# Gated graph network, 2048 nodes: the first two chunks' gates as block products over both chunks, and operands loaded one by one

## The chip, the cores and the metric

One NeuronCore of one Trainium2 chip. The metric is the device time of one execution in microseconds, the median of the runs shown.

## What is computed

Five steps of a gated graph network on 2048 nodes with 256 features, then a small head, a residual and a layer norm. Each step is, with A the 0/1 adjacency matrix:

```
a_in  = A   @ (state @ in_W.T  + in_b)
a_out = A.T @ (state @ out_W.T + out_b)
a = concat([a_in, a_out, state])
r = sigmoid(a @ r_W.T + r_b);  z = sigmoid(a @ z_W.T + z_b)
h_hat = tanh(concat([a_in, a_out, r * state]) @ h_W.T + h_b)
state = (1 - z) * state + z * h_hat
```

The end is out = layernorm(x + tanh(state @ o1_W.T + o1_b) @ o2_W.T + o2_b).

## The kernel before, in words

The input and output weights are folded into the gates' weights, so a step is an adjacency part, y = A state and A.T state, and a gate part. The state stands transposed in `state_t`: two feature tiles of 128 rows, 2048 nodes in columns, in four chunks of 512 (chunks 0 to 3). All arithmetic that must be exact to fp32 is split into a high and a low f16 half: a product is then three passes over (high, high), (high, low), (low, high), `PASSES`. The biases that pass through A become a degree row times a vector; ScalarE seeds a gate's PSUM bank with one direction's (`seed`, L490) and VectorE adds the other's (`degree_part`, L831).

**Adjacency part (steps 1 to 4).** Four groups a step: group g has direction g % 2 (0 is A.T, which feeds the second weight block) and chunk pair g // 2. A group multiplies a 2 x 2 block matrix by a 2 x 2 block matrix with seven block products instead of eight (Strassen's scheme in Winograd's form). The products are named P1, P6, P5, P7, P3, P2, P4 after their semaphores, in TensorE's order in `group`; each is 16 matmuls 128 x 128 by 128 x 512 (`product`, L1173) from the turned state rows `xop` and the fp8 matrix block sums. ScalarE copies P1 (L536), VectorE adds the products up to the four corners y11, y22, y12, y21 (L1012 to L1031), and each corner is split into halves by ScalarE (`y_hi`, L554) and VectorE (`y_lo`, L1038). P1, P2 share bank A; P6, P7, P4 bank B; P5 has bank E, P3 bank C. `first_group` is group 0 of a step in another order, since the state rows of chunk 3 reach `xop` last: 36 matmuls on the early rows, 4 of P1, 12 of P3, P2, 4 of P6, 4 of P5, P7, 4 of P3, P4. P2 there waits for the copy of P1, P7 for VectorE's first sum.

**Operands.** The seven matrix block sums of each group lie in DRAM (`kept`, 3.67 MB a group). Each of two SBUF places holds a whole group: SP (`load_group`, L310) loads group at + 2 in two DMAs when P4 of group at is done. SP also issues the DMA transposes that turn new state rows into `xop` (`turn_rows`, L324), in the same queue. In step 0 the raw blocks were stored by SP (`store_raw`, L301 and L303).

**Gate part.** `gates(t, c)` for one chunk: six tiles (r, z, h by two feature tiles), each of 6 blocks x 3 passes = 18 matmuls (`gate_tile`, L1260), in three banks in turn. ScalarE applies sigmoid or tanh (L476), VectorE forms r * state (L837), z's part and the new state (L848, L854, L857). Beside the last tiles of a chunk the next chunk's banks are seeded, in the last chunk (c = 3) those of the next step. The new state is split for the gates (`split_hi` L447, `split_lo` L777), and its rows and the block sums of them are split for the transposes (`rows_hi` L464, L468; `row_sums` L821 to L826; `rows_lo` L803 to L810).

**Order of a step.** first_group, group 1, gates of chunks 0 and 1, groups 2 and 3, gates of chunks 2 and 3. Every engine's program is written out by hand in that order, and each engine works strictly in its order.

Of the kernel before, what the change touches and what calls it, by code (L numbers as in the profile page):

```python
# [15 lines left out]
P = 128  # L16
N = 2048
D = 256
STEPS = 5
# [29 lines left out]
Y_SPLIT = {False: {"y22": 1, "y12": 2, "y11": 3, "y21": 4}, True: {"y11": 1, "y22": 2, "y12": 3, "y21": 4}}  # L49
# [6 lines left out]
def gnn_program(nc, x, x_t, adj, adj_t, io_w, gate_w, o_w, bias, o2_b, out):  # L56
    ctx = ExitStack()
    with ctx:
# [6 lines left out]
        def need(eng, s, value):  # L65
            if value > 0:
# [11 lines left out]

        tg_words = PAIRS * NX * CW // 4
        slot_w = [areg[:, d * half:d * half + tg_words].rearrange("p (m w) -> p m w", m=PAIRS) for d in range(2)]  # L80
        slot8 = [areg[:, d * half:d * half + tg_words].bitcast(F8).rearrange("p (m s n) -> p m s n", m=PAIRS, s=NX)
                 for d in range(2)]
# [22 lines left out]
        sum_1, sum_u, sum_v = [pq_words[:, slot_words + i * CW:slot_words + (i + 1) * CW] for i in range(3)]  # L105
# [14 lines left out]
        rs16 = tmp[:, 6 * CW:8 * CW].bitcast(F16).rearrange("p (s f n) -> p s f n", s=2, f=FT)  # L120
        ring_b = tmp[:, 8 * CW:12 * CW].rearrange("p (r w) -> p r w", r=2)
# [7 lines left out]
        vdeg = sb("vdeg", [P, 2, GT], F32)  # L129
        mx = sb("mx", [P, 12], F32)  # L130
# [9 lines left out]
        gate_bank = bank[4:7]  # L140

# [23 lines left out]
        s_slot = [sem("s_slot0"), sem("s_slot1")]  # L165
        s_p1, s_p6, s_p5, s_p7, s_p3, s_p2, s_p4 = [sem(f"s_prod{i}") for i in (1, 6, 5, 7, 3, 2, 4)]
        s_sum1, s_sumu, s_u4, s_sumv = sem("s_sum1"), sem("s_sumu"), sem("s_u4"), sem("s_sumv")
        s_y22, s_y12, s_y21 = sem("s_y22"), sem("s_y12"), sem("s_y21")
        s_yh, s_yl = sem("s_yh"), sem("s_yl")
        s_gate = sem("s_gate")  # L170
# [21 lines left out]
        def pq_slot(t, c):  # L192
            return c if t == 0 else 2 + c % 2
# [66 lines left out]
        def _(sp):  # L260
# [45 lines left out]
            def load_group(t, g):  # L306
                d = g % 2
                for h in range(2):
                    ms = slice(h * PAIRS // 2, (h + 1) * PAIRS // 2)
                    sp.dma_start(slot_w[d][:, ms, :], kept[g][:, ms, :]).then_inc(s_slot[d], 16)  # L310
# [23 lines left out]
            load_group(1, 0)  # L334
# [9 lines left out]
            load_group(1, 1)  # L344
            for t in range(1, STEPS):
                for g in range(4):
                    at = 4 * (t - 1) + g
                    if at + 2 < 4 * LAST:
# [1004 lines left out]
```

## Time and profile before

| | us |
|---|---|
| median of 3 runs | 1029.72 |
| lowest, highest | 1029.61, 1030.45 |
| the profiled execution | 1030.75 |
| its span | 1028.9 |
| TensorE busy in the span | 1005.5 (98%) |
| VectorE busy | 592.3 (58%) |
| ScalarE busy | 403.8 (39%) |
| granted TensorE clock, mean | 0.992 of full |

The span runs from the first to the last instruction of one profiled execution; the profiled execution's own time lies 1.85 us above its span. A matmul's listed duration overlaps its neighbours'; what counts is the distance from one start to the next.

### The profile page before, as it was taken

The page shows a single profiled execution, that of the slowest core. Times are in us where ns is not written, and L with a number is a line of the kernel's source. Part 1 is how long each engine was busy: PE and PEld are TensorE (multiplying, and loading weights), DVE is VectorE, ACT ScalarE, POOL GpSimd, SP SyncE. Part 2 cuts the span into 40 slices and gives each one's busy share as a digit, 9 for nine tenths or more (in the row PEclk, how much of TensorE's full clock was granted, in tenths as well). Part 3 has the DMA queues.
Part 4 walks back from the last instruction along what each step waited for, and adds up shares of the span by engine and source line. Part 5 has one row for each costly group of instructions (what it writes and reads, how often), then busy time and mean ns, then how long its engine had stood idle before and what let it go on. Part 6 is the DMA issues. An engine that isn't in the chain of part 4 may idle for free.

```text
span 1028.9 us, 11463 instructions
## 1 busy us (share of the span) xinstructions
PE 1005.5 (98%) x4648; PEld 458.5 (45%) x4648; DVE 592.3 (58%) x933; ACT 403.8 (39%) x544; POOL 38.7 (4%) x43
## 2 busy tenths in 40 slices
PE   6999999999999999999999999999999999999995
PEld 3444444444444444444444444444444444444443
DVE  4999968895354338544433674353347534446756
ACT  3656665542144126413421552143135314322443
POOL 0311000000000000000000000000000002001100
PEclk8999999999999999999999999999999999999998
DMA  9998991327430244333003642410344335001101
GB/s 330 389 411 344 396 343 33 77 65 218 151 136 0 103 166 91 72 143 143 1 1 143 189 72 72 169 73 0 143 154 72 62 143 189 1 1 42 42 1 41
DMA packets 87236, 134.30 MB, mean 131 GB/s; under 512 B 60432, under 2 KB 75408, under 8 KB 78992
## 3 DMA queue, kind: packets, MB, share of 16 engines
q1 hardware_dynamic: 84880, 125.19, 35.8%
q0 software_dynamic: 2304, 8.39, 2.1%
q8 instruction: 36, 0.59, 0.2%
q14 instruction: 16, 0.13, 0.0%
HBM read 102.11 MB, written 16.78 MB: 116 GB/s over the span
## 4 chain that ended last, share of the span: by engine, by line
PE 92%; DVE 3%; ACT 2%; DMA 1%; issue 1%; SPq 1%; ACTq 0%; DVEq 0%
PE bank L1260 42%; PE bank L1173 36%; PE bank L1116 11%; PE bank L1292 1%; DMA tmp<-in_adj 1%; PE bank L1273 1%; DMA xop_words<-pq_words 0%; SPq L270 0%; DVE pq_words L810 0%; ACT pq_words L468 0%; DVE pq_words L1012 0%; DVE areg L957 0%; ACT pq_words L554 0%; ACT tmp L476 0%; DVE tmp L704 0%
## 5 line engine op out<-in xcount | busy, mean ns | idle before, releaser
L1173 PE MATMUL bank<-areg,xop_words 128*128 128x512 fp8e4 x1792 | 390.1, 379 | 1.4 <-DVE pq_words L1012 1.1
L1260 PE MATMUL bank<-pq_words,w 128*128 128x512 f16 x1440 | 327.3, 379 | 0.0
L1173 PEld LDWEIGHTS bank<-areg,xop_words 128*128 128x128 f16 x1792 | 174.5, 98 | 214.7 <-DVE pq_words L1012 3.1
L1260 PEld LDWEIGHTS bank<-pq_words,w 128*128 128x128 f16 x1440 | 140.9, 98 | 169.9 <-DVE pq_words L1038 0.2
L476 ACT ACTIVATE tmp<-bank,bias_sb,scal 128x512 f32<-128x512 f32 x120 | 93.1, 776 | 201.4 <-PE bank L1260 201.4
L554 ACT ACTIVATE pq_words<-pq_words 128x512 f16<-128x512 f32 x48 | 30.2, 630 | 236.8 <-DVE pq_words L1024 140.5
L831 DVE SCALAR_TENSOR_TENSOR bank<-deg_words,vdeg,bank 128x512 f32<-128x512 f16 x120 | 90.0, 752 | 51.8 <-ACT bank L490 50.7
L1260 PE MATMUL bank<-split,w 128*128 128x512 f16 x480 | 116.7, 379 | 2.4 <-issue 1.9
L1116 PE MATMUL bank<-areg,xop_words 128*128 128x512 fp8e4 x512 | 113.5, 385 | 3.7 <-ACT areg L421 3.7
L490 ACT ACTIVATE bank<-deg_words,vdeg 128x512 f32<-128x512 f16 x120 | 82.7, 691 | 5.2 <-DVE deg_words L794 1.5
L1116 PEld LDWEIGHTS bank<-areg,xop_words 128*128 128x128 f16 x512 | 50.7, 99 | 66.0 <-issue 7.4
L421 ACT ACTIVATE areg<-tmp 128x2048 fp8e4<-128x2048 int32 x32 | 61.1, 1910 | 37.3 <-DMA tmp<-in_adj_t 18.9
L1260 PEld LDWEIGHTS bank<-split,w 128*128 128x128 f16 x480 | 46.7, 98 | 59.7 <-issue 2.4
L1260 PE MATMUL bank<-tmp,w 128*128 128x512 f16 x240 | 58.3, 379 | 0.0
L837 DVE TENSOR_TENSOR tmp<-tmp,state_t 128x512 f32<-128x512 f32 x40 | 27.6, 690 | 51.4 <-ACT tmp L476 51.3
L1038 DVE SCALAR_TENSOR_TENSOR pq_words<-pq_words 128x512 f16<-128x512 f32 x48 | 33.2, 692 | 33.4 <-ACT pq_words L554 33.4
L854 DVE TENSOR_TENSOR tmp<-tmp 128x512 f32<-128x512 f32 x40 | 27.6, 690 | 38.5 <-ACT tmp L476 38.5
L404 POOL TENSOR_TENSOR areg<-areg,diag_words 128x256 f32<-128x256 f32 x16 | 15.8, 1020 | 724.4 <-DMA areg<-in_x 724.4
L1038 DVE SCALAR_TENSOR_TENSOR pq_words<-bank,pq_words 128x512 f16<-128x512 f32 x16 | 11.1, 691 | 53.7 <-ACT pq_words L554 53.7
L777 DVE SCALAR_TENSOR_TENSOR split<-state_t,scal,split 128x1024 f16<-128x1024 f32 x23 | 30.1, 1308 | 13.7 <-ACT split L447 13.7
L1260 PEld LDWEIGHTS bank<-tmp,w 128*128 128x128 f16 x240 | 23.5, 98 | 28.3
L482 ACT ACTIVATE tmp<-tmp,scal 128x512 f16<-128x512 f32 x40 | 28.9, 722 | 11.2 <-DVE tmp L837 9.9
(132 smaller groups left out, 602.9 us busy)
## 6 DMA issues: line engine op xcount, KB each, us to landing
areg<-kept_operands SPq DMA_DIRECT2D x32, 1792.0 KB, 10.6
tmp<-in_adj SPq DMA_DIRECT2D x16, 1024.0 KB, 7.0
tmp<-in_adj_t SPq DMA_DIRECT2D x16, 1024.0 KB, 8.3
kept_operands<-xop_words POOLq DMA_DIRECT2D x11, 512.0 KB, 8.2
areg<-in_x SPq DMA_DIRECT2D x8, 512.0 KB, 8.1
kept_operands<-areg SPq DMA_DIRECT2D x4, 1024.0 KB, 10.2
kept_operands<-tmp POOLq DMA_DIRECT2D x5, 512.0 KB, 3.3
pq_words<-in_gate_w SPq DMA_DIRECT2D x6, 384.0 KB, 6.2
```

The costliest lines, as they stand in the source:

```text
L421: nc.scalar.activation(raw8[k // JT][:, k % JT, :], stage[:, k % STG, :], ACT.Copy, accum_out=degc[:, k // JT, k % JT:k % JT + 1], saturat ...
L476: nc.scalar.activation(dst[:, gi % FT, :], gate_bank[gi % 3][:, :], ACT.Tanh if gi >= 2 * FT else ACT.Sigmoid, bias=bias_sb[:, 4 + gi:5 + ...
L482: nc.scalar.activation(rs16[:, 0, f, :], r_buf[:, f, :], ACT.Identity, scale=SIG).then_inc(s_rsh, 1)
L490: nc.scalar.activation(gate_bank[gi % 3][:, :], deg[:, 0, cols(c)], ACT.Identity, scale=vdeg[:, 0, gi:gi + 1]).then_inc(s_c0, 1)
L554: nc.scalar.activation(dst, src, ACT.Copy, scale=PSC / XDOWN).then_inc(s_yh, 1)
L777: nc.vector.scalar_tensor_tensor(split[:, c % 2, 1, :, :], state_t[:, :, cols(c)], SIG, split[:, c % 2, 0, :, :], ALU.mult, ALU.subtract). ...
L831: nc.vector.scalar_tensor_tensor(slot, deg[:, 1, cols(c)], vdeg[:, 1, gi:gi + 1], slot, ALU.mult, ALU.add).then_inc(s_c1, 1)
L837: nc.vector.tensor_tensor(r_buf[:, f, :], r_buf[:, f, :], state_t[:, f, cols(c)], ALU.mult) \
L1038: nc.vector.scalar_tensor_tensor(rows[:, 1, :], src, PSC / XDOWN, rows[:, 0, :], ALU.mult, ALU.subtract).then_inc(s_yl, 1)
L1116: return nc.tensor.matmul(dst[:, :], state_n[:, j, part, feat(f)], adj8[:, j, cols(c)], start=j == 0 and part == 0, stop=j == JT - 1 and p ...
L1173: last = nc.tensor.matmul(dst[:, :], xop[:, m // 2, operand_block(xo, part, m % 2), :], slot8[g % 2][:, m, mo, :], start=first and m == pa ...
L1260: last = nc.tensor.matmul(dst[:, :], w16[:, k, wp, feat(gi)], rhs, start=False, stop=i == KT - 1 and (wp, xp) == PASSES[-1], skip_group_ch ...
```

## The change

For chunks 0 and 1 of steps 1 to 4 (groups 0 and 1) the gates' adjacency input is formed for both chunks together. For each gate (r, z, h) the weights (two blocks by two feature tiles) times y (two blocks by two chunks) is again a 2 x 2 block product, by the same seven-product scheme. Four banks hold the four output tiles. The products on the right need y11, y21, y22 and four sums t1 to t4 of y's corners, which VectorE now forms in each of the two groups; seven instead of four values are split into halves (`Y_ORDER`), y12 no longer. The weights' block sums (`ws`) are formed once, in step 1: VectorE adds high and low of a direction's weights (`weight_full`, 1536 elements a partition), forms four sums of 384, ScalarE rounds them to f16 (`weight_hi`, 1536), VectorE makes the low halves. The degree terms are seeded per bank, two of them with differences (`vdif`, `degd`). Inside a gate VectorE adds the four products up to the corner banks while TensorE goes on with the rest; ScalarE copies the first product and one sum. The state parts stay as they are, 6 matmuls a tile. States of chunks 0 and 1 are both split between groups 0 and 1. All splits now use one scale.

The matrix operands have one SBUF place each instead of two for whole groups; the second region holds the split y values. SP loads each operand of the next group (512 KB, in pieces of 512 B) as soon as the product that used it is done. The last chunk of a step no longer seeds the next step's banks; the banks of chunk 2 are seeded in group 3.

`Y_ORDER` is y11, y22, t1, t3, t2, y21, t4 in group 0 and y22, t3, y11, t1, t2, y21, t4 in group 1. The core of the diff:

```diff
+            def load_operand(at, mo, done):
+                if at > 0:
+                    sp.wait_ge(done, at)
+                sp.dma_start(place_w[:, mo, :, :], kept[at % 4][:, :, mo * CW // 4:(mo + 1) * CW // 4]) \
+                    .then_inc(s_place[mo], 16)
+            def load_group(at):
+                load_operand(at, M11, s_p1)
+                load_operand(at, MT2, s_p6)
...
-                        sp.wait_ge(s_p4, at + 1)
-                        load_group(t + (g + 2) // 4, (g + 2) % 4)
+                for at in range(4 * (t - 1) + 1, 4 * t + 1):
+                    if at < 4 * LAST:
+                        load_group(at)
...
-                    elif n + 1 < CH * STEPS and n + 1 != CH * LAST + 2:
-                        seed(n + 1, (c + 1) % CH, gi - 3)
+                    elif c < CH - 1:
+                        seed(n + 1, c + 1, gi - 3)
...
+                copy_p1(t, g)
+                if g == 1:
+                    for i in range(4):
+                        pair_seed(t, 0, i)
...
+                if g == 3:
                     for gi in range(2):
                         seed(CH * t + 2, 2, gi)
...
+                for name in Y_ORDER[g]:
+                    if t == 1 and g == 1 and name == "y11":
+                        weight_hi(1)
+                    y_hi(t, g, name)
+                    if g == 1 and name == "y21":
+                        pair_copy(t, 0)
...
+            def pair_gates(t):
+                pair_seed(t, 1, 0)
+                pair_base_21(t, 0)
+                for i in range(1, 4):
+                    pair_seed(t, 1, i)
+                for i in range(3):
+                    pair_act(t, 0, i)
+                    pair_reset_hi(t, i)
+                pair_act(t, 0, 3)
+                pair_copy(t, 1)
...
                 rows_hi(n, 1)
+                if t == 1:
+                    weight_hi(0)
                 group(t, 0)
-                split_hi(0, split_at(t, 0), CH * (t - 1) + 1)
+                split_hi(0, split_at(t, 0), CH * (t - 1) + 2)
+                split_hi(1, split_at(t, 1), CH * (t - 1) + 2)
                 group(t, 1)
-                gates(t, 0)
-                gates(t, 1)
+                pair_gates(t)
...
-                ahead = n + 1 < CH * STEPS and n + 1 != CH * LAST + 2
+                ahead = c < CH - 1
...
+                elif name == "t1":
+                    dve.wait_ge(s_yh, y_done(t, g, "y11"))
+                    dve.wait_ge(s_y12, at + 1)
+                    if g == 1:
+                        dve.wait_ge(s_d3, pair_at + 1)
+                    nc.vector.tensor_tensor(y_sum_at[g]["t1"], sum_u, bank_a[:, :], ALU.subtract).then_inc(s_d1, 1)
+                elif name == "t2":
+                    dve.wait_ge(s_d1, pair_at + 1)
+                    nc.vector.tensor_tensor(y_sum_at[g]["t2"], sum_v, y_sum_at[g]["t1"], ALU.subtract).then_inc(s_d2, 1)
...
+            def weight_full(d):
+                k = FT * (1 - d)
+                if d == 0:
+                    dve.wait_ge(s_gate, GT * CH)
+                else:
+                    dve.wait_ge(s_wsh, 1)
+                nc.vector.tensor_tensor(w_full, w16[:, k:k + FT, 0, :], w16[:, k:k + FT, 1, :], ALU.add) \
...
+                nc.vector.tensor_tensor(s1, a21, a22, ALU.add).then_inc(s_wsum, 1)
...
+                nc.vector.tensor_tensor(degd, deg[:, :, cols(1)], deg[:, :, cols(0)], ALU.subtract).then_inc(s_gdeg, 1)
...
+                if t == 1 and g == 1:
+                    weight_full(1)
...
                 sums_v(at)
-                y_sum(at, "y22")
+                if t == 1 and g == 1:
+                    weight_sums(1)
+                if g == 1:
+                    for i in range(4):
+                        pair_degree(t, 0, i)
+                y_sum(t, g, "y22")
                 y_lo(t, g, "y22")
-                y_sum(at, "y12")
+                y_sum(t, g, "y12")
+                if g < 2:
+                    if g == 0:
+                        y_sum(t, g, "t1")
+                        y_sum(t, g, "t3")
+                        y_lo(t, g, "t1")
+                        y_lo(t, g, "t3")
+                    else:
+                        y_sum(t, g, "t3")
+                        y_lo(t, g, "t3")
+                        if t == 1:
+                            weight_lo(1)
+                        y_sum(t, g, "t1")
+                        y_lo(t, g, "y11")
+                        y_lo(t, g, "t1")
+                    y_sum(t, g, "t2")
+                    y_lo(t, g, "t2")
+                    y_sum(t, g, "y21")
+                    y_sum(t, g, "t4")
+                    y_lo(t, g, "y21")
+                    y_lo(t, g, "t4")
+                    return
...
+            def pair_sum_u(t, gate):
+                unit, slots = 3 * (t - 1) + gate, pair_banks[gate]
+                dve.wait_ge(s_gp6, unit + 1)
+                dve.wait_ge(s_gs1, unit + 1)
+                nc.vector.tensor_tensor(sum_b, slots[1][:, :], sum_a, ALU.add).then_inc(s_gu, 1)
+            def pair_sum_12(t, gate):
+                unit, slots = 3 * (t - 1) + gate, pair_banks[gate]
+                dve.wait_ge(s_gp5, unit + 1)
+                dve.wait_ge(s_gu, unit + 1)
+                nc.vector.tensor_tensor(slots[1][:, :], slots[2][:, :], sum_b, ALU.add).then_inc(s_g12, 1)
+            def pair_sum_22(t, gate):
+                unit, slots = 3 * (t - 1) + gate, pair_banks[gate]
+                dve.wait_ge(s_gp7, unit + 1)
+                nc.vector.tensor_tensor(sum_a, slots[3][:, :], sum_b, ALU.add).then_inc(s_gv, 1)
+                dve.wait_ge(s_gv, unit + 1)
+                nc.vector.tensor_tensor(slots[2][:, :], slots[2][:, :], sum_a, ALU.add).then_inc(s_g22, 1)
...
+            def pair_gates(t):
+                pair_sum_u(t, 0)
+                pair_sum_12(t, 0)
+                pair_sum_22(t, 0)
+                pair_degree(t, 1, 0)
+                pair_degree(t, 1, 1)
+                pair_degree(t, 1, 2)
+                pair_degree(t, 1, 3)
+                for i in range(3):
+                    pair_reset(t, i)
+                    pair_reset_lo(t, i)
+                pair_reset(t, 3)
+                pair_sum_u(t, 1)
...
+                if t == 1:
+                    degree_differences()
+                    weight_full(0)
+                    weight_sums(0)
+                    weight_lo(0)
                 group(t, 0)
                 split_lo(0, split_at(t, 0))
+                split_lo(1, split_at(t, 1))
...
+                pe.wait_ge(s_place[mo], 16 * (at + 1))
...
+                if g == 1:
+                    pe.wait_ge(s_d1, 2 * (t - 1) + 1)
+                elif g == 2:
+                    pe.wait_ge(s_zh, FT * CH * t + 1)
+                else:
+                    pe.wait_ge(s_yl, y_done(t, 2, "y11"))
+                product(bank_a, at, X11, M11, every).then_inc(s_p1, 1)
                 need(pe, s_y21, at)
-                product(bank_b, g, XS2, MT2, every).then_inc(s_p6, 1)
+                if g == 2:
+                    pe.wait_ge(s_zh, FT * CH * t + 2)
+                product(bank_b, at, XS2, MT2, every).then_inc(s_p6, 1)
...
+            def pair_product(t, gate, dst, operand, weights):
+                for d in range(2):
+                    if gate == 0:
+                        pe.wait_ge(s_yl, y_done(t, d, [n for n in Y_PLACE if Y_PLACE[n] == operand][0]))
+                        if t == 1 and operand in (Y22, YT1, YT2, YT3):
+                            pe.wait_ge(s_wsl, d + 1)
+                    for wp, xp in PASSES:
+                        last = nc.tensor.matmul(dst[:, :], weights(d, wp), yop[:, d, operand, xp, :], start=False,
+                                                stop=False, skip_group_check=True)
+                return last
...
+                pe.wait_ge(s_c1, seeds + 1)
+                pair_product(t, gate, slots[0], Y11, block(0, 0)).then_inc(s_gp1, 1)
+                pe.wait_ge(s_c1, seeds + 2)
+                pair_product(t, gate, slots[1], YT2, block_sum(2)).then_inc(s_gp6, 1)
+                pe.wait_ge(s_c1, seeds + 3)
+                pair_product(t, gate, slots[2], YT1, block_sum(1)).then_inc(s_gp5, 1)
+                pe.wait_ge(s_c1, seeds + 4)
+                pair_product(t, gate, slots[3], YT3, block_sum(3)).then_inc(s_gp7, 1)
+                pe.wait_ge(s_gs1, unit + 1)
+                pair_product(t, gate, slots[0], Y21, block(0, 1))
+                pair_state(t, gate, 0)
+                pe.wait_ge(s_g12, unit + 1)
+                pair_product(t, gate, slots[1], Y22, block_sum(4))
+                pair_state(t, gate, 1)
+                pe.wait_ge(s_g22, unit + 1)
+                pair_state(t, gate, 2)
+                pe.wait_ge(s_g21, unit + 1)
+                pair_product(t, gate, slots[3], YT4, block(1, 1))
+                pair_state(t, gate, 3)
```

## Rows read from the trace of the kernel before

**Rows 1.** The page: busy time of TensorE, and the chain by engine.
```profile
PE 1005.5 (98%) x4648; PEld 458.5 (45%) x4648; DVE 592.3 (58%) x933; ACT 403.8 (39%) x544; POOL 38.7 (4%) x43
...
PE 92%; DVE 3%; ACT 2%; DMA 1%; issue 1%; SPq 1%; ACTq 0%; DVEq 0%
```

**Rows 2.** The chain of waits in order of time: start, us, what; step 1.
```profile
281.71 46.62 PE bank L1260 x216
328.33 48.35 PE bank L1173 x224
```

**Rows 3.** TensorE's waits: us in total, times, longest.
```profile
PE bank L1173 <- DVE pq_words L1012: 1.1, 4, 0.3
```

**Rows 4.** The chain of waits before step 1's first group.
```profile
225.46 0.69 ACT bank L490
...
233.53 0.66 DVE bank L831
```

**Rows 5.** TensorE's timeline: start, us, line, operation, count, idle before and what ended it.
```profile
21.20 110.62 PE L1116 MATMUL bank<-areg,xop_words 128*128 128x512 fp8e4 x500 [3.69 <-ACT areg L421]
...
138.18 1.46 PE L1260 MATMUL bank<-split,w 128*128 128x512 f16 x6 [1.90 <-issue]
...
232.22 7.93 PE L1173 MATMUL bank<-areg,xop_words 128*128 128x512 fp8e4 x36
240.40 8.81 PE L1173 MATMUL bank<-areg,xop_words 128*128 128x512 fp8e4 x40 [0.25 <-DMA xop_words<-pq_words]
```

**Rows 6.** VectorE's timeline at the end of step 0.
```profile
237.34 0.42 DVE L821 TENSOR_TENSOR diag_words<-state_t 128x256 f32<-128x256 f32 x1
...
238.47 0.42 DVE L826 TENSOR_TENSOR diag_words<-state_t,diag_words 128x256 f32<-128x256 f32 x1
...
240.51 1.28 DVE L810 SCALAR_TENSOR_TENSOR pq_words<-diag_words,scal,pq_words 128x1024 f16<-128x1024 f32 x1
```

**Rows 7.** Groups by line and shape, VectorE, then ScalarE: busy us, mean ns.
```profile
L707 DVE TENSOR_TENSOR xop_words<-areg 128x1024 fp8e4<-128x1024 fp8e4 x11 | 13.4, 1217 | 0.0
...
L421 ACT ACTIVATE areg<-tmp 128x2048 fp8e4<-128x2048 int32 x32 | 61.1, 1910 | 37.3 <-DMA tmp<-in_adj_t 18.9 <-DMA tmp<-in_adj 18.4
...
L447 ACT ACTIVATE split<-state_t,scal 128x1024 f16<-128x1024 f32 x23 | 26.1, 1133 | 0.4 <-DVE state_t L857 0.4
...
L536 ACT COPY pq_words<-bank 128x512 f32<-128x512 f32 x16 | 9.4, 585 | 26.0 <-PE bank L1173 26.0
```

**Rows 8.** Windows: stretch, length, busy of each engine, granted clock, DMA share, GB/s.
```profile
21.00:23.00 2.00, 1.80 (x5) 0.74 (x6) 1.96 (x5) 2.00 (x6) 0.00 (x0) 0.50 0.97 332
...
25.00:27.00 2.00, 2.00 (x8) 0.82 (x7) 2.00 (x5) 1.35 (x2) 0.00 (x0) 0.66 1.01 376
...
138.00:140.00 2.00, 1.82 (x9) 0.90 (x10) 2.00 (x5) 1.98 (x5) 0.00 (x0) 1.00 1.02 305
```

**Rows 9.** VectorE's timeline at the end of step 2's first group.
```profile
443.64 0.69 DVE L1024 TENSOR_TENSOR pq_words<-bank,pq_words 128x512 f32<-128x512 f32 x1 [2.53 <-PE bank L1173]
445.03 0.69 DVE L1038 SCALAR_TENSOR_TENSOR pq_words<-pq_words 128x512 f16<-128x512 f32 x1 [0.70 <-ACT pq_words L554]
445.64 0.68 DVE L1028 TENSOR_TENSOR pq_words<-bank,pq_words 128x512 f32<-128x512 f32 x1
...
448.06 0.69 DVE L1031 TENSOR_TENSOR pq_words<-bank,pq_words 128x512 f32<-128x512 f32 x1 [0.35 <-PE bank L1173]
```

**Rows 10.** ScalarE's timeline, the same place.
```profile
444.37 0.63 ACT L554 ACTIVATE pq_words<-pq_words 128x512 f16<-128x512 f32 x1 [5.77 <-DVE pq_words L1024]
```

**Rows 11.** SP's storing of one raw matrix block, 512 KB in 512 B pieces.
```profile
L301 SPq DMA_DIRECT2D kept_operands<-areg x4: 983/2513/4620, 116.6 to 133.2; - x4
...
DMA to landing us min/median/max: 8.5/9.7/12.5
```

**Rows 12.** Windows: the stretch of those stores, and step 1's groups.
```profile
127.00:138.00 11.00, 9.28 (x43) 3.85 (x41) 7.67 (x21) 6.85 (x13) 0.00 (x0) 1.00 1.07 362
...
232.20:281.70 49.50, 48.96 (x226) 21.77 (x225) 22.17 (x33) 10.29 (x15) 0.72 (x1) 1.00 0.54 185
```

More of the change, by code:

```diff
@@ L47 @@
 NX = 7
-Y_SPLIT = {False: {"y22": 1, "y12": 2, "y11": 3, "y21": 4}, True: {"y11": 1, "y22": 2, "y12": 3, "y21": 4}}
+Y11, Y21, Y22, YT1, YT2, YT3, YT4 = range(7)
+Y_ORDER = {0: ("y11", "y22", "t1", "t3", "t2", "y21", "t4"), 1: ("y22", "t3", "y11", "t1", "t2", "y21", "t4"),
+           2: ("y22", "y12", "y11", "y21"), 3: ("y22", "y12", "y11", "y21")}
+Y_BASE = (0, 7, 14, 18)
+Y_STEP = 22
+Y_PLACE = {"y11": Y11, "y21": Y21, "y22": Y22, "t1": YT1, "t2": YT2, "t3": YT3, "t4": YT4}
+PAIR_TILES = ((0, 0), (0, 1), (1, 1), (1, 0))
 TJOBS = [(d, m) for d in range(2) for m in range(PAIRS)]
@@ L164, in gnn_program @@
         s_raw = [sem("s_raw0"), sem("s_raw1")]
[L165 removed]
+        s_place = [sem(f"s_place{i}") for i in range(NX)]
         s_p1, s_p6, s_p5, s_p7, s_p3, s_p2, s_p4 = [sem(f"s_prod{i}") for i in (1, 6, 5, 7, 3, 2, 4)]
@@ L565, in group @@
-                y_hi(t, g, "y22")
-                y_hi(t, g, "y12")
-                if g > 0:
-                    y_hi(t, g, "y11")
-                y_hi(t, g, "y21")
-                if t == LAST and g == 3:
-                    seed(CH * t + 2, 2, 2)
+                for name in Y_ORDER[g]:
[4 more added lines that the diff above has]
+                        pair_copy(t, 0)
@@ L1055, in group, with pair_degree @@
                 y_lo(t, g, "y12")
-                if g > 0:
-                    y_lo(t, g, "y11")
-                if t == LAST and g >= 2:
+                y_lo(t, g, "y11")
+                if t == LAST:
                     residual(g - 2)
-                y_sum(at, "y21")
+                y_sum(t, g, "y21")
                 y_lo(t, g, "y21")
-                if t == LAST and g == 3:
+                if g == 3:
                     degree_part(CH * t + 2, 2, 2)
+            def pair_degree(t, gate, i):
+                slot = pair_banks[gate][i][:, :]
+                row, scale = pair_term(gate, i, 1)
+                dve.wait_ge(s_c0, GT * CH * t + 4 * gate + i + 1)
+                nc.vector.scalar_tensor_tensor(slot, row, scale, slot, ALU.mult, ALU.add).then_inc(s_c1, 1)
@@ L1217, in first_group @@
                 need(pe, s_y12, at)
-                product(bank_c, g, XS4, M22, early, final=False)
+                product(bank_c, at, XS4, M22, early, final=False)
                 pe.wait_ge(s_sum1, at + 1)
-                product(bank_a, g, X12, M21, every, first=False).then_inc(s_p2, 1)
+                product(bank_a, at, X12, M21, every, first=False).then_inc(s_p2, 1)
                 wait_turned(pe, 1, n)
-                product(bank_b, g, XS2, MT2, late, first=False).then_inc(s_p6, 1)
@@ L1227, in first_group @@
+                product(bank_c, at, XS4, M22, late, first=False).then_inc(s_p3, 1)
                 pe.wait_ge(s_y22, at + 1)
-                product(bank_b, g, X22, MT4, every, first=False).then_inc(s_p4, 1)
+                product(bank_b, at, X22, MT4, every, first=False).then_inc(s_p4, 1)
             def ready(t, c, k):
@@ new lines, in pair_state @@
+            def pair_state(t, gate, i):
+                f, c = PAIR_TILES[i]
+                gi = FT * gate + f
+                if gate == 0:
+                    pe.wait_ge(s_spl, split_at(t, c) + 1)
+                if gate == 2:
+                    pe.wait_ge(s_rsl, FT * CH * t + 4)
+                for k in range(FT):
+                    for wp, xp in PASSES:
+                        rhs = split[:, c, xp, k, :] if gate < 2 else rs_pair[:, c, xp, k, :]
+                        last = nc.tensor.matmul(pair_banks[gate][i][:, :], w16[:, 2 * FT + k, wp, feat(gi)], rhs,
+                                                start=False, stop=k == FT - 1 and (wp, xp) == PASSES[-1],
+                                                skip_group_check=True)
+                last.then_inc(s_gate, 1)
@@ L1314, in _ @@
                 group(t, 1)
-                gates(t, 0)
-                gates(t, 1)
+                for gate in range(3):
+                    pair_gate(t, gate)
                 group(t, 2)
```

343 lines of the change are left out of this document (259 added, 84 removed).

## The prediction

> **What bounds the kernel now.** I read the page's busy shares and chain first, then TensorE's waits, the chain by time, and the timelines of the engines beside it. TensorE is busy 98% of the span and holds 92% of the chain [rows 1]: this kernel is a stream of matmuls. In steps 1 to 4 the chunk-pair gates run 216 matmuls in 46.62 us without a gap, 0.2158 us from start to start, and two adjacency groups 224 in 48.35 us, the same pace [rows 2]. (A matmul is listed with 379 ns since neighbours overlap; the pace counts.) In the adjacency groups a VectorE sum holds TensorE up in four places, 1.1 us in all [rows 3]. So a matmul taken away is worth 0.2158 us, and the question is whether VectorE and ScalarE, with the work they are given for it, still keep ahead of TensorE.
>
> **Matmuls removed.** A pair of chunks took 2 x 6 gate tiles x 6 blocks x 3 passes = 216 matmuls. Now each of three gates takes four products of 2 directions x 3 passes (24), three more (18), and four state parts of 6 (24): 66, so 198 a pair. 18 fewer in each of four steps are 72 x 0.2158 = **15.5 us less**.
>
> **Seeds no longer made ahead in the last chunk's gates.** In step 0 the chain from the last state rows to the first group runs over such a seed on ScalarE and such a degree part on VectorE [rows 4] to the transpose that TensorE waits for: 36 matmuls from 232.22 would end at 239.99, the next starts at 240.40, a gap of 0.41 us [rows 5]. Without the two pieces (0.69 and 0.66 us, partly beside other waits) I make the rows 0.8 us earlier, so the gap goes: **0.4 us less**. In steps 1 to 4 that work is moved to beside the adjacency groups, where there are 3 us of slack.
>
> **Weight sums, first direction (step 1 only).** ScalarE's copy of the first product now stands behind its rounding of the weight sums, and that behind VectorE's making them; the product X12 x M21 waits for that copy. VectorE, from its last row piece (starts 240.51, 1.28 us long, now 0.8 earlier, ends 240.99) [rows 6]: two tiny differences 0.25; one of 1024 elements 1.14 and the weights' hi plus lo of 1536 elements 1.75 (by 1217 ns for 1024 and 0.42 us for 256 [rows 6, 7], some 1.04 ns an element; successors start 0.08 before an end); four sums of 384, where the four of 256 take from 237.34 to 238.89, 1.55, and 128 more elements each make 2.08. That ends at 246.2. ScalarE's 1536 elements cost 1.52 (1133 ns for 1024 and 1910 for 2048), the copy 0.58 [rows 7]: TensorE goes on at 248.3. It is ready after 36 + 4 + 12 matmuls, at 243.4. **4.8 us more.** From both sides: 3.4 if the f16 sources run faster than the rows of fp8 and f32, 5.9 if nothing comes earlier; I take the rows' own rate. The Trainium skill (VectorE: DVE Perf Modes, The perf-mode tier table) gives tensor_tensor on 16-bit data in SBUF twice the rate of fp32; by it the 1024-element f16 difference would cost some 0.5 us less and the stall would be 4.3. No row here has that form.
>
> **TensorE's clock after that stall.** After 3.69 us idle (to 21.2 us) the granted clock was 0.50, that is 1.2 GHz, until between 25 and 27 us (0.66 there), so about 5.2 us at half rate; after the 1.90 us idle to 138.18 it was 1.00 [rows 5, 8]. A stall of 4.8 us is beyond the first. Half of 5.2: **2.6 us more**; bounds 0 (the clock stays) and 3.4.
>
> **Seven splits instead of four in an adjacency group.** VectorE's tail of a group is a chain with ScalarE: a sum (0.69), ScalarE's high half (0.63), the low half, each 0.04 after its source; independent VectorE instructions start 0.61 apart, dependent ones so 0.73 [rows 9, 10]. On step 2's clock, first group: the y22 sum starts at 443.64 as before, its low half 445.03, the y12 sum 445.64. Then t1 446.36 to 447.05, t3 447.09, low t1 447.75, low t3 448.47, t2 449.08, low t2 (its high half ends 450.44) 450.47, and only then the y21 sum, 451.08 to 451.77. P7 ends at some 443.5, 4 + 16 matmuls behind it make 447.8; there group 1 begins (bank A is free before, at 447.05), and its second product wants bank B after 16 more, at 451.3. It must wait for the y21 sum, which formerly began at 448.06 [rows 9]. The wait is 0.5 us, in four steps **2.0 us more**; bounds 0 and 1.2 each. In group 1 what follows has cover: both state splits (some 1.2 us each by 1024 elements [rows 7], the second moved here from the gates) delay the first sum to 457.3, wanted at 458.7; four degree parts (0.66 us apart [rows 4]) end by 462.8, where product P7 ends at 462.2 and its sum is wanted at 469.1.
>
> **The gates begin without a cushion.** They began with six state matmuls and six of the first direction; now the second direction's y11 is their fourth matmul and t2 their tenth. Group 1 ends at 472.5. Low y11 is ready at 471.2, t2 at 474.0, wanted at 474.4: 0.4 us of cover. The first product's copy (475.8, wanted 477.7), low y21 (476.0), the first corner sum (478.5, wanted 480.3) have 2 us each. I followed the other two gates likewise: each runs 14.2 us, its copy and sums come 2 to 3 us early, seeds earlier still. The group behind waits for the second update's first product, which is over 2 us early. Cost 0, but where VectorE ran 1 us later in this stretch, each step would lose about 0.6.
>
> **Weight sums, second direction (step 1).** In group 1 VectorE also has 1.75 + 2.08 and, late, the low halves, 1.75; ScalarE 1.52. The y22 sum then comes 2.4 us after its product, and the low halves of the weights stand before t1. Low y11 is 0.2 us late, low t2 comes at 476.1 instead of 474.0, 1.5 us late after that: **1.7 us more**, bounds 0 and 3.2.
>
> **Operands in seven loads.** Same bytes, in pieces of 512 B instead of rows of 14 KB, issued by SP as each product ends. Nothing of before loads this way; the nearest row is SP's storing of 512 KB in 512 B pieces, median 2.51 us of SP and 9.7 us to landing, longest 4.62 [rows 11]. The hardest place is the first group, where six of the seven loads, P6's first, are issued only when P6 is done, after 36 + 4 + 12 + 16 + 4 = 72 matmuls or 15.5 us. With 2.5 us each the last issue starts at 28.0 and lands at 37.7; it is wanted when group 1 has done six products: 24.2 + 0.3 (the group's old wait) + 0.5 + 20.7 = 45.7. Cost 0. The transposes of state rows stand behind a load that waits for the same last product as before. The second group's early load disappears, nothing waits for that.
>
> **Sum.** -15.5 - 0.4 + 4.8 + 2.6 + 2.0 + 1.7 = -4.8 us. The profiled execution took 1030.75 us (span 1028.9), now 1025.9. The median of three runs is 1.03 below that execution: 1029.72 - 4.8 = **1024.9 us**.
>
> **Rivals.**
> - *The step-1 stall is short and the clock stays up* (chance 0.15). For it: 16-bit sources may go faster, and the clock held through 1.9 us. Against: two thirds of the stall would have to go, or the fall of the clock at 3.69 us be chance. Without clock loss 1022.3, with the lower stall too 1020.9.
> - *The gates wait for their own sums* (0.13). Three gates in four steps hang on a ping-pong of ScalarE and VectorE that stood off the path. For it: both queues are in order, and a reset stands between copy and sums. Against: 2 us of cover. A wait of 0.4 us in each of 12 gates gives 4.8 back: 1029.7, no change.
> - *Operand loads come late; slower* (0.06). If each load holds SP 4.62 us, the sixth is issued at 15.5 + 5 x 4.62 = 38.6 and lands 9.7 later at 48.3, where 45.7 is wanted: 2.6 us in each step, 10.4 in all, 1035.3. It decides from 4.45 us a load on, where 1.7 us in each step make 1031.8, 0.2% above before. Against: the 4.62 was met among other stores, at a DMA share of 1.07, where the groups of step 1 have 0.54 [rows 12]. The Trainium skill (DMA: Bandwidth & Descriptors, Bandwidth) wants 1 MiB in a DMA for 75% of peak, which speaks against loads of 512 KB; by its 138 GB/s for 64 KB as the worst case, an estimate is 3.8 us a load, still in time. No row here has this load.
> - *The weight sums hide after all* (0.04): then the step-1 terms vanish and it is 1015.8.
>
> My forecast has 0.62. A difference under 0.2% (2.1 us) is about what a measurement of this kernel can't tell from none. Faster takes the forecast, the first and the last rival, less a tail of the forecast (its high bounds together reach +6): 0.8. Same 0.12, slower 0.08. For 8 in 10 the range goes from the first rival's short end, 1020.5, to nearly the second rival's, 1029.
>
> **What would show it.** 198 matmuls in a pair's gates at an unchanged pace, 42.7 us; a gap of TensorE in step 1's first group of 3.4 to 5.9 us, ended by ScalarE's copy, with a granted clock of 0.5 behind it; 0.5 us before group 1's second product in every step, ended by VectorE's y21 sum; 1.7 us in step 1's first gate, by low y11 and t2. Waits for a load, or gaps at the gates' later products in steps 2 to 4, would make it wrong; so would a gate stretch of over 43.5 us in steps 2 to 4.

## The result

| | before | changed |
|---|---|---|
| median, us | 1029.74 (4 runs) | 1036.41 (4 runs) |
| lowest to highest | 1029.61 to 1030.45 | 1035.56 to 1037.22 |
| the profiled execution, its span | 1030.75, 1028.9 | 1037.02, 1035.2 |

The ratio is 1.0063, 95% interval 1.0046 to 1.0081: the changed kernel is slower, where 1024.9 us was forecast.

The page of the changed kernel: span, busy times, and the chain by engine.

```profile
span 1035.2 us, 11766 instructions
...
PE 993.9 (96%) x4576; PEld 450.9 (44%) x4576; DVE 666.0 (64%) x1052; ACT 425.4 (41%) x594; POOL 35.3 (3%) x43
...
PE 79%; DVE 12%; ACT 3%; issue 3%; DMA 2%; SPq 1%; POOL 0%; ACTq 0%; DVEq 0%; POOLq 0%
```

TensorE has 72 matmuls fewer and is busy 11.6 us less, yet the span is longer, and TensorE's share of the chain fell from 92% [rows 1] to 79%. Its waits, in us in total, times, longest:

```profile
PE bank L1499 <- DVE pq_words L1188: 13.3, 5, 11.1
...
PE bank L1499 <- ACT pq_words L604: 3.9, 1, 3.9
...
PE bank L1610 <- DVE areg L1215: 1.3, 1, 1.3
PE bank L1499 <- DVE pq_words L1168: 1.1, 4, 0.3
```

Four of the five sums named L1188 (y21) are the short waits before group 1's second product, the copy L604 is step 1's first group, L1215 is step 1's first gate, and L1168 is the wait that stood there before [rows 3]. The fifth L1188 is one wait of 11.1 us, which no term of the prediction had. TensorE's timeline has it in the last step:

```profile
912.11 13.98 PE L1499 MATMUL bank<-areg,xop_words 128*128 128x512 fp8e4 x64
937.17 5.32 PE L1499 MATMUL bank<-areg,xop_words 128*128 128x512 fp8e4 x16 [11.08 <-DVE pq_words L1188]
942.32 2.75 PE L1668 MATMUL bank<-split,o 128*128 128x512 f16 x12
```

64 matmuls from 912.11 end at 925.92; the next 16, product P6 of group 3, start at 937.17, 11.25 us later, and take until 942.32, 5.15 us where 3.45 is their pace, so 1.7 us more. P6 wants bank B, and VectorE's y21 sum of group 2 holds it. VectorE's timeline there, then GpSimd's, then SP's:

```profile
919.85 0.69 DVE L1215 SCALAR_TENSOR_TENSOR areg<-bank,areg 128x512 f16<-128x512 f32 x1 [2.00 <-ACT areg L636]
933.42 0.88 DVE L1110 SCALAR_TENSOR_TENSOR areg<-bank,scal,areg 128x256 f32<-128x256 f32 x2 [12.88 <-POOL areg L467]
...
936.42 0.69 DVE L1188 TENSOR_TENSOR pq_words<-bank,pq_words 128x512 f32<-128x512 f32 x1
```

```profile
930.62 5.49 POOL L467 TENSOR_TENSOR areg<-areg,diag_words 128x256 f32<-128x256 f32 x8 [697.48 <-DMA areg<-in_x]
```

```profile
896.73 26.45 SPq L366 DMA_DIRECT2D areg<-kept_operands  x7
923.23 0.66 SPq L419 DMA_DIRECT2D diag_words<-in_o_b  x1
923.94 0.97 SPq L423 DMA_DIRECT2D areg<-in_x  x2
```

VectorE had its last low half of group 2 at 919.85 and stood idle for 12.9 us before the residual of chunk 0 (L1110), which stands before the y21 sum (L1188). The residual needs x plus o2_b, which GpSimd adds when x has landed, and SP issued x at 923.94, behind seven operand loads that follow one another from 896.73: each waits for a product of group 2, the last for P4, which is group 2's end. Before, SP issued the same loads of x right behind the last group load, 72 us ahead of the residual, and the residual followed VectorE's last low half (926.53) at once:

```profile
854.66 1.10 SPq L360 DMA_DIRECT2D areg<-in_x  x2
```

```profile
927.14 0.86 DVE L957 SCALAR_TENSOR_TENSOR areg<-bank,scal,areg 128x256 f32<-128x256 f32 x2
```

The rest of the new waits are those forecast. Step 1 on TensorE, then the VectorE and ScalarE instructions that end the waits:

```profile
230.41 11.39 PE L1499 MATMUL bank<-areg,xop_words 128*128 128x512 fp8e4 x52
245.66 8.04 PE L1499 MATMUL bank<-areg,xop_words 128*128 128x512 fp8e4 x24 [3.86 <-ACT pq_words L604]
253.99 11.49 PE L1499 MATMUL bank<-areg,xop_words 128*128 128x512 fp8e4 x52 [0.29 <-DVE pq_words L1168]
265.96 20.89 PE L1499 MATMUL bank<-areg,xop_words 128*128 128x512 fp8e4 x96 [0.48 <-DVE pq_words L1188]
...
288.04 0.81 PE L1610 MATMUL bank<-areg,pq_words 128*128 128x512 f16 x3
290.16 3.41 PE L1610 MATMUL bank<-areg,pq_words 128*128 128x512 f16 x15 [1.31 <-DVE areg L1215]
```

```profile
239.14 0.68 DVE L1249 TENSOR_TENSOR pq_words<-deg_words 128x1024 f16<-128x1024 f16 x1
239.74 1.75 DVE L1225 TENSOR_TENSOR tmp<-w 128x1536 f32<-128x1536 f16 x1
...
243.06 0.56 DVE L1238 TENSOR_TENSOR tmp<-tmp 128x384 f32<-128x384 f32 x1
...
289.41 0.69 DVE L1215 SCALAR_TENSOR_TENSOR areg<-pq_words,areg 128x512 f16<-128x512 f32 x1 [0.70 <-ACT areg L636]
```

```profile
243.65 1.47 ACT L640 CAST pq_words<-tmp 128x1536 f16<-128x1536 f32 x1 [6.29 <-DVE tmp L1238]
245.03 0.58 ACT L604 COPY pq_words<-bank 128x512 f32<-128x512 f32 x1
```

The granted clock in three stretches (length, busy time of each engine, clock, DMA share, GB/s): one behind step 1's gap, two behind the 11 us.

```profile
245.60:250.00 4.40, 4.34 (x11) 1.59 (x12) 1.31 (x1) 0.00 (x1) 0.00 (x0) 0.50 0.17 51
...
937.00:939.00 2.00, 1.83 (x5) 0.74 (x6) 0.96 (x3) 1.85 (x3) 0.00 (x0) 0.50 0.00 0
...
942.00:946.00 4.00, 4.00 (x21) 1.77 (x19) 3.33 (x12) 1.53 (x3) 0.00 (x0) 1.00 0.38 126
```

### The profile page after: what moved, and what is told of

It is laid out like the page before. It is cut to its first block, busy times and chain, and to the rows that moved or that the text cites. A ratio compares the mean times of both kernels' runs of the same rounds, so it can differ in the third digit from the quotient of the medians.

```text
span 1035.2 us, 11766 instructions
## 1 busy us (share of the span) xinstructions
PE 993.9 (96%) x4576; PEld 450.9 (44%) x4576; DVE 666.0 (64%) x1052; ACT 425.4 (41%) x594; POOL 35.3 (3%) x43
## 4 chain that ended last, share of the span: by engine, by line
PE 79%; DVE 12%; ACT 3%; issue 3%; DMA 2%; SPq 1%; POOL 0%; ACTq 0%; DVEq 0%; POOLq 0%
PE bank L1499 31%; PE bank L1597 24%; PE bank L1610 10%; PE bank L1625 6%; PE bank L1441 5%; DMA areg<-in_x 2%; ACT areg L636 1%; PE bank L1687 1%; PE bank L1668 1%; DVE scal L829 1%; DVE xop_words L806 1%; DVE w L839 1%; DVE pq_words L963 0%; DMA xop_words<-pq_words 0%; DVE areg L1215 0%
## 5 line engine op out<-in xcount | busy, mean ns | idle before, releaser
L636 ACT ACTIVATE areg<-pq_words 128x512 f16<-128x512 f32 x72 | 45.4, 630 | 237.0 <-DVE pq_words L1181 118.4
L1597 PE MATMUL bank<-areg,w 128*128 128x512 f16 x576 | 131.0, 379 | 0.0
L540 ACT ACTIVATE tmp<-bank,bias_sb,scal 128x512 f32<-128x512 f32 x72 | 55.8, 775 | 104.1 <-PE bank L1597 104.1
L1597 PEld LDWEIGHTS bank<-areg,w 128*128 128x128 f16 x576 | 56.4, 98 | 68.0 <-DVE areg L1215 0.2
L1215 DVE SCALAR_TENSOR_TENSOR areg<-pq_words,areg 128x512 f16<-128x512 f32 x72 | 49.8, 692 | 32.7 <-ACT areg L636 31.9
L1610 PE MATMUL bank<-areg,pq_words 128*128 128x512 f16 x288 | 66.3, 379 | 1.3 <-DVE areg L1215 1.3
L1597 PE MATMUL bank<-pq_words,w 128*128 128x512 f16 x288 | 65.4, 379 | 0.0
L984 DVE SCALAR_TENSOR_TENSOR bank<-deg_words,vdeg,bank 128x512 f32<-128x512 f16 x72 | 53.6, 752 | 18.2 <-ACT bank L556 17.7
L1610 PE MATMUL bank<-areg,w 128*128 128x512 f16 x216 | 52.6, 379 | 0.0
L556 ACT ACTIVATE bank<-deg_words,vdeg 128x512 f32<-128x512 f16 x72 | 49.2, 690 | 3.3 <-DVE deg_words L947 1.5
L1597 PEld LDWEIGHTS bank<-pq_words,w 128*128 128x128 f16 x288 | 28.2, 98 | 34.0
L1215 DVE SCALAR_TENSOR_TENSOR areg<-bank,areg 128x512 f16<-128x512 f32 x16 | 11.0, 690 | 47.5 <-ACT areg L636 47.5
L930 DVE SCALAR_TENSOR_TENSOR split<-state_t,scal,split 128x1024 f16<-128x1024 f32 x23 | 29.2, 1287 | 13.7 <-ACT split L511 13.7
```

Source lines behind the costliest of these rows:

```text
L540: nc.scalar.activation(dst[:, gi % FT, :], gate_bank[gi % 3][:, :], ACT.Tanh if gi >= 2 * FT else ACT.Sigmoid, bias=bias_sb[:, 4 + gi:5 + ...
L556: nc.scalar.activation(gate_bank[gi % 3][:, :], deg[:, 0, cols(c)], ACT.Identity, scale=vdeg[:, 0, gi:gi + 1]).then_inc(s_c0, 1)
L636: nc.scalar.activation(y_dst(g, name)[:, 0, :], src, ACT.Copy, scale=PSC).then_inc(s_yh, 1)
L930: nc.vector.scalar_tensor_tensor(split[:, c % 2, 1, :, :], state_t[:, :, cols(c)], scale, split[:, c % 2, 0, :, :], ALU.mult, ALU.subtract ...
L984: nc.vector.scalar_tensor_tensor(slot, deg[:, 1, cols(c)], vdeg[:, 1, gi:gi + 1], slot, ALU.mult, ALU.add).then_inc(s_c1, 1)
L1215: nc.vector.scalar_tensor_tensor(rows[:, 1, :], src, PSC, rows[:, 0, :], ALU.mult, ALU.subtract).then_inc(s_yl, 1)
```

## The experiments

The profiled executions are compared from the start of the first gate matmul to the end, as the front part of the program, which none of the edits is about, ended between 136.4 and 138.7 us. That length is 890.7 us before (1028.9 - 138.2), 898.8 changed. It comes from one execution of each kernel; the medians stand beside it.

**e1_early_x.** One edit in the changed kernel, on SP:

```diff
+            def residual_input(c):
+                sp.dma_start(y[:, c % 2, :, :], x_v[:, c * JC:(c + 1) * JC, :]).then_inc(s_xr[c % 2], 16)
             for t in range(1, STEPS):
+                if t == LAST:
+                    sp.wait_ge(s_xl, 2 * CH * LAST)
+                    sp.dma_start(b2_all, o2_b.partition_broadcast(P)).then_inc(s_b2, 16)
+                    for c in range(2):
+                        residual_input(c)
                 for at in range(4 * (t - 1) + 1, 4 * t + 1):
...
-            sp.wait_ge(s_xl, 2 * CH * LAST)
-            sp.dma_start(b2_all, o2_b.partition_broadcast(P)).then_inc(s_b2, 16)
             for c in range(CH):
                 if c >= 2:
                     sp.wait_ge(s_out[c % 2], 32)
-                sp.dma_start(y[:, c % 2, :, :], x_v[:, c * JC:(c + 1) * JC, :]).then_inc(s_xr[c % 2], 16)
+                    residual_input(c)
```

> The changed kernel with one edit: SP issues the loads of o2_b and of x for chunks 0 and 1 at the start of step 4, before the operand loads of its groups, not after them. Theory (SP's queue): in the last step SP's program reaches the load of x only after the load that waits for group 2's last product; VectorE's residual of chunk 0 waits for x, and the y21 sum stands behind it, which TensorE wants for group 3's second product. Then the gap there (11.3 us from the time it was wanted, and 1.7 us at half clock behind it) goes whole: the changed kernel's 1036.4 less 13.0, 1023.4 us, and VectorE's y21 sum of group 2 ends some 1.8 us before TensorE wants bank B. Rival (VectorE's own load: more splits and sums push the y21 sum out): the gap stays, 1036.4. Rival (small pieces: the operand loads fill the DMA queues, so x lands late wherever it is issued, or the operands do in its place): x still lands over 6 us after its issue and a wait of several us for it or for an operand remains, 1028 or more.

Measured: 1024.07 us against 1030.43 of before in the same runs, ratio 0.9937 (0.9924 to 0.9950). The length is 885.1 us, 13.7 less than the changed kernel's. VectorE's and TensorE's timelines at the place:

```profile
919.65 0.69 DVE L1221 SCALAR_TENSOR_TENSOR areg<-bank,areg 128x512 f16<-128x512 f32 x1 [2.00 <-ACT areg L642]
920.26 0.87 DVE L1116 SCALAR_TENSOR_TENSOR areg<-bank,scal,areg 128x256 f32<-128x256 f32 x2
...
923.25 0.69 DVE L1194 TENSOR_TENSOR pq_words<-bank,pq_words 128x512 f32<-128x512 f32 x1
```

```profile
911.91 17.43 PE L1505 MATMUL bank<-areg,xop_words 128*128 128x512 fp8e4 x80
```

The residual (L1116) follows the low half at once, the y21 sum (L1194) ends at 923.94, and TensorE runs 80 matmuls through where it had stopped after 64. The end of P6's predecessor is 911.91 + 13.81 = 925.72, so the cover is 1.8 us. The order of SP's program is the cause. The gap and its clock loss make 13.0 of the 13.7; of the rest, step 1's clock loss was 1.0 less in this execution (7.3 us for 24 matmuls instead of 8.3), and the program's last stretch 0.2 longer. The other waits are unchanged.

**b1_late_x.** The kernel before with one wait more:

```diff
             sp.wait_ge(s_xl, 2 * CH * LAST)
+            sp.wait_ge(s_p4, 4 * LAST - 1)
             sp.dma_start(b2_all, o2_b.partition_broadcast(P)).then_inc(s_b2, 16)
```

> The kernel before with one wait added: SP waits for the last product of group 2 in step 4 before it loads o2_b and x. Nothing else of the change is in it. Theory (SP's queue alone makes the loss): VectorE's residual of chunk 0 waits for x, the y21 sum behind it, and TensorE's second product of group 3 starts some 11 us late, with 1.7 us lost at half clock: 1029.7 + 13, 1042.7 us. Rival (the loss needs the change's other work on VectorE or the small loads): less than half of that, under 1036.

**b2_loads** and **b3_loads_early_x.** The operands' part of the change alone, in the kernel before (gates, seeds and splits as before); b3 has e1's edit too.

```diff
-                    if at + 2 < 4 * LAST:
-                        sp.wait_ge(s_p4, at + 1)
-                        load_group(t + (g + 2) // 4, (g + 2) % 4)
+                for at in range(4 * (t - 1) + 1, 4 * t + 1):
+                    if at < 4 * LAST:
+                        load_group(at)
...
+                pe.wait_ge(s_place[mo], 16 * (at + 1))
```

> The kernel before, its gates untouched, with the operands' part of the change alone: one place for each operand, seven loads of 512 KB in 512 B pieces as each product ends, x loaded behind them. Theory: the same loss as with the wait added, 1042.7, since the order in SP's program is the same. Rival (the small pieces cost something by themselves): more than that, with TensorE waits for operand loads in groups 1 or 3.

> The same operands' part in the kernel before, with x loaded at the start of step 4. Theory: loads in small pieces are free, each lands over 10 us before it is wanted: 1029.7, within 0.1%. Rival (small pieces cost): over 1031, with waits of TensorE for operand loads.

| | us | ratio to before | length from first gate |
|---|---|---|---|
| b1_late_x | 1040.71 | 1.0106 (1.0093 to 1.0120) | 900.8 |
| b2_loads | 1042.66 | 1.0133 (1.0116 to 1.0150) | 902.7 |
| b3_loads_early_x | 1029.71 | 1.0003 (0.9994 to 1.0012) | 890.9 |

SP's issue of x and TensorE's timeline in b1, then in b2, where the 64 matmuls start at 917.86 too:

```profile
928.84 0.98 SPq L361 DMA_DIRECT2D areg<-in_x  x2
```

```profile
917.86 13.98 PE L1174 MATMUL bank<-areg,xop_words 128*128 128x512 fp8e4 x64
940.54 5.04 PE L1174 MATMUL bank<-areg,xop_words 128*128 128x512 fp8e4 x16 [8.70 <-DVE pq_words L1032]
```

```profile
929.69 1.77 SPq L365 DMA_DIRECT2D areg<-in_x  x2
```

```profile
942.47 5.04 PE L1179 MATMUL bank<-areg,xop_words 128*128 128x512 fp8e4 x16 [10.63 <-DVE pq_words L1036]
```

The same wait arises in a kernel whose gates were never touched. With SP's wait alone it is 8.9 us (940.54 less 917.86 + 13.81), and the clock loss 1.4; with the operand loads 10.8, and the clock loss 1.4 again. The 1.9 us between them are the loads' own: x is issued 0.85 us later, and GpSimd, which waits for it, starts 6.22 us after the issue (935.91) instead of 5.15 (933.99 in b1). So the expected 13 came out as 11.2 in b1 by the medians, well over the rival's 1036, and b2 gave the 1042.7 that was expected. b3 shows no wait for an operand, only the two known ones:

```profile
PE bank L1185 <- DVE pq_words L1023: 1.1, 4, 0.3
...
PE bank L1185 <- DMA xop_words<-pq_words: 0.3, 1, 0.3
```

Loading in pieces of 512 B costs nothing that 11 runs can tell.

**e2_copy_first, e3_y21_first, e4_all.** All have e1's edit. e2 puts the copy first and the low halves later:

```diff
                 copy_p1(t, g)
+                if t == 1 and g == 0:
+                    weight_hi(0)
...
                 rows_hi(n, 1)
-                if t == 1:
-                    weight_hi(0)
                 group(t, 0)
...
                 sums_v(at)
+                if t == 1 and g == 0:
+                    weight_lo(0)
...
                     weight_sums(0)
-                    weight_lo(0)
```

> As the kernel with x loaded early, and in step 1 ScalarE copies P1 before it rounds the first direction's weight sums; VectorE makes their low halves after its first three group sums instead of before. Theory (TensorE waits for the copy behind the rounding, and loses clock after it): the gap of 4.0 us in step 1's first group goes, and the 2.7 us that 24 matmuls lose at the granted clock of 0.50 with it, 6.7 us in all: 1016.7. Rival (the low halves or the full weights then delay the next sums): a gap of 1 to 3 us remains at P7 or P4 of the first group. Rival (the clock falls for another reason): the gap goes but the matmuls after it still show 0.50, then 4.0 us less only, 1019.4.

e3 forms the y21 sum earlier in group 0:

```diff
+                    if g == 0:
+                        y_sum(t, g, "y21")
                     y_sum(t, g, "t2")
                     y_lo(t, g, "t2")
-                    y_sum(t, g, "y21")
+                    if g == 1:
+                        y_sum(t, g, "y21")
```

> As the kernel with x loaded early, and in group 0 of each step VectorE forms the y21 sum before t2 and its low half, not after. Theory (the second product of group 1 waits only because the y21 sum stands at the end of VectorE's tail): the gap of 0.5 to 0.8 us before that product goes in all four steps, the y21 sum starting when P4 is done or when the low half of t3 is issued; 2.3 us less than with x loaded early alone, 1021.1. Rival (the tail as a whole is too long, so t2 or t4, now later, meet TensorE elsewhere): the time moves by under 0.5 us, and the wait shows again at the gates' t2 or at P7 of group 1.

e4 has both and moves the second direction's weight sums (shown are the new places, VectorE's first; the old ones go):

```diff
                     weight_sums(0)
+                    weight_full(1)
...
                 sums_u(t, g)
+                if t == 1 and g == 1:
+                    dve.wait_ge(s_wsh, 1)
+                    weight_sums(1)
...
                     for i in range(4):
                         pair_degree(t, 0, i)
+                    if t == 1:
+                        weight_lo(1)
...
                         pair_seed(t, 0, i)
+                    if t == 1:
+                        weight_hi(1)
```

> All three (x early, y21 sum first, copy first), and the second direction's weight sums moved forward: full weights in a free stretch of VectorE before group 0's sums, sums before group 1's second sum, rounding behind the bank seeds, low halves before the y22 sum. Theory: 1023.4 - 6.7 - 2.3, and the 1.5 us of step 1's first gate go too: 1012.9. Since 72 matmuls less are worth 15.5 and the first group's old gap 0.4, that is all of it but 1 us. Rival (the slack of VectorE in group 1 is used up): the sum of the parts is not reached, 1014 to 1016, with the rest of the wait at step 1's first gate or at P4 of group 1.

| | us | ratio to before | length from first gate |
|---|---|---|---|
| e1_early_x | 1024.07 | 0.9937 (0.9924 to 0.9950) | 885.1 |
| e3_y21_first | 1022.63 | 0.9925 (0.9912 to 0.9938) | 882.3 |
| e2_copy_first | 1018.39 | 0.9886 (0.9871 to 0.9901) | 879.2 |
| e4_all | 1014.26 | 0.9841 (0.9827 to 0.9855) | 873.7 |

e2's TensorE shows no gap before 248.55, and behind it only the y21 wait and the gate's:

```profile
248.55 11.49 PE L1506 MATMUL bank<-areg,xop_words 128*128 128x512 fp8e4 x52 [0.29 <-DVE pq_words L1174]
260.52 20.89 PE L1506 MATMUL bank<-areg,xop_words 128*128 128x512 fp8e4 x96 [0.48 <-DVE pq_words L1194]
...
284.72 3.41 PE L1617 MATMUL bank<-areg,pq_words 128*128 128x512 f16 x15 [1.30 <-DVE areg L1221]
```

Its length is 5.9 us under e1's. e1 had the gap of 4.0 us (ScalarE's wait is listed as 3.9) and lost 1.7 us in the 24 matmuls behind it; both are gone, 5.7. The expected 6.7 had the changed kernel's 2.7 us of clock loss in it, of which e1 had 1.7. In e3 VectorE's two rows at step 2 are the y21 sum and then t2:

```profile
454.30 0.69 DVE L1194 TENSOR_TENSOR pq_words<-bank,pq_words 128x512 f32<-128x512 f32 x1
454.90 0.68 DVE L1208 TENSOR_TENSOR pq_words<-pq_words 128x512 f32<-128x512 f32 x1
```

The wait is gone in all four steps; the gaps were 0.65, 1.0, 0.65 and 0.65 us (idle plus the 0.16 by which a last matmul's listed time overlaps), 3.0 in all. Against them stand a new wait of 0.45 us for low y11 at step 1's gates and 0.8 us more clock loss in step 1 (8.1 us for the 24 matmuls, e1 7.3), and for them 1.1 us less in the program's last stretch, which was not edited: 2.8. So the edit is worth 2.5 us by its waits. The medians show 1.4, between the theory's 2.3 and the rival's 0.5, and the intervals of the two ratios overlap: the size rests on this one trace, and the wait that the rival saw come back at the gates is there with 0.45 of the 3.0 us only. e4 is left with the waits that before had:

```profile
PE bank L1697 <- DVE areg L1116: 3.3, 1, 3.3
...
PE bank L1509 <- DVE pq_words L1174: 1.1, 4, 0.3
```

```profile
span 1011.3 us, 11767 instructions
...
PE 986.9 (98%) x4576; PEld 450.3 (45%) x4576; DVE 665.2 (66%) x1052; ACT 425.9 (42%) x594; POOL 35.3 (3%) x43
```

TensorE is busy 98% again, with 72 matmuls fewer. From the first gate to the end of TensorE's last gap (L1697, 3.3 us) it takes 862.3 us, before 878.4: 16.1 less, where the matmuls and step 1's old gap make 15.9. The last stretch behind that gap, not edited, ran 11.4 us instead of 12.3. Its 24 matmuls ran at a granted clock of 1.00 here and took 2.79 us; before they took 4.27 at 0.65, behind the same gap:

```profile
999.89 2.79 PE L1697 MATMUL bank<-o,pq_words 128*128 128x256 f16 x24 [3.33 <-DVE areg L1116]
```

The median of e4, 1014.26, lies 1.4 above its forecast and in the range of its rival, used-up slack. But the waits that the rival named, at step 1's first gate or at P4 of group 1, are not in the trace. The forecast began 0.7 us under what e1 came to, and took off the changed kernel's 2.7 us of clock loss, of which e1 had 1.7: together 1.7, which would cover it.

## Why the prediction was wrong, by its steps

- **What bounds the kernel** was right: the pace stayed 0.2158 us, and each matmul taken away counted once no wait stood against it.
- **Matmuls removed, 15.5 us less**: right. A pair's gates take 198 matmuls and 42.74 us in step 2, forecast 42.7; the chain there has the end of group 1, the gates' first piece and the next group:

```profile
455.11 20.89 PE bank L1499 x96
476.00 6.47 PE bank L1610 x30
...
518.74 48.35 PE bank L1499 x224
```

- **Seeds not made ahead, 0.4 us less**: right; the 52 matmuls from 230.41 run without a gap.
- **Weight sums, first direction, 4.8 us more**: the place and the releaser were right, the size was 4.0 (241.63 to 245.66). The term that was too large is the degree difference, put at 1.14 us up to the next instruction's start and 0.60 in the trace (0.68 listed); pieces of 0.1 us and less make the rest. The 1536 elements of the weights took 1.75 as forecast. The range's low end of 3.4 had both fast. The Trainium skill (VectorE: DVE Perf Modes, The perf-mode tier table) gives tensor_tensor on 16-bit data in SBUF twice the rate of fp32. The trace agrees for the difference, 0.68 us for 1024 elements; the weights, f16 sources with an f32 result, took 1.75 us for 1536, the single rate.
- **Clock after it, 2.6 us more**: 2.7 in the changed kernel (8.33 us from 245.66 to 253.99, of which 5.18 is the matmuls' pace and 0.46 the old wait), at a granted clock of 0.50. e1 lost 1.7, b1 1.4 behind 8.9 us: the loss varies by the execution. The forecast 2.6 met the changed kernel's 2.7 with some luck.
- **Seven splits, 2.0 us more**: 3.0. The chain was as laid out; two dependent hand-overs inside VectorE took 0.79 us from start to start instead of 0.73, and in step 2 one took 1.14. A wait that is the small difference of two long chains needs the links' spread in its size.
- **Gates without a cushion, 0**: right in steps 2 to 4. **Second direction, 1.7 us more**: 1.5.
- **Operands in seven loads, 0**: right as far as it went. The sizes were far better than the bound: SP needs 0.52 us a load and it lands 4.3 us after its issue, where 2.51 and 9.7 were taken from the stores [rows 11]:

```profile
L366 SPq DMA_DIRECT2D areg<-kept_operands x112: 517/518/3221, 135.9 to 922.7; - x112
...
DMA to landing us min/median/max: 4.0/4.3/9.3
```

**The operand loads are the step that failed.** It asked who waits for the operands and who for the transposes behind them, and said of the removed early load that nothing waits for that. What stands behind the last load in SP's program is the load of o2_b and x. Before, SP's last load waited for P4 of the second group of step 4; now it waits for P4 of the third, one group and a pair of gates later. The consumer is not TensorE but VectorE's residual, and behind that, in VectorE's order, the y21 sum. 11.25 + 1.7 us, as large as all the gain.
- **The sum**: with the measured terms -15.5 - 0.4 + 4.0 + 2.7 + 3.0 + 1.5 = -4.7, where -4.8 was forecast. That they agree to 0.1 us is luck: 0.8 too much for the weight sums stands against 1.0 too little for the splits. With the 12.95 us missed it is +8.2, and the lengths from the first gate differ by 8.1. The profiled execution is 6.3 slower, as its front part was 1.8 us shorter. e1, which is the change without the missed wait, came to 0.9937 of before, which is 1023.3 against the forecast 1024.9.
- **The rivals**: the slow end was given to late operand loads with 0.06. The queue was the right one, the victim the wrong one: the loads were early enough and what stood behind them was not. The gates waiting for their own sums did not occur; the weights were not hidden; the clock did fall.

## What to carry to other kernels

When a wait is put into an in-order queue, go through everything that the queue issues afterwards to the end of the program, not only what the change is about: a load that was issued 72 us early can lose all its lead, and it shows at an instruction of another engine that has nothing to do with it. One-off preparation belongs behind the instruction that TensorE waits for, even if it was written ahead of it: here moving a copy in front of a rounding gave 5.9 us. And of two results that an engine forms at a group's end, the one that frees a bank comes first.

## What the runs showed of the hardware

A VectorE subtraction of 1024 elements with f16 sources and f16 result took 0.68 us, against 1.22 for fp8 [rows 7]; f32 took 0.68 for 512 elements. With f16 sources and an f32 result 1536 took 1.75, the single rate.

512 KB loaded from DRAM in 512 B pieces held SP for 0.52 us and landed in 4.3 in the median, while the stores in the same pieces took 2.51 and 9.7. The direction is not all of it: the first seven of the same loads, issued from 135.92 right behind the stores, held SP for 1.40 to 3.22 us and landed in 7.3, with the DMA engines' share at 1.02 falling to 0.87 (0.43 from 897 to 923 us). An issue time measured while the DMA engines are full says little of one at a share of 0.43.

The half-rate stretch behind a TensorE gap of 4 us cost 1.7 to 2.7 us, and behind gaps of 8.9, 10.8 and 11.25 us no more, 1.4, 1.4 and 1.7. Behind the last gap, 3.33 or 3.34 us idle in every kernel here, it cost nothing in e4 and 1.3 to 2.5 us in the eight others (24 matmuls in 2.79 us, and in 4.12 to 5.30).
